# Four rounds of 32 batches in place of five, the routing score moved to GpSimd and PSUM, and a new order of steps

## What is computed

```python
ctx = causal_ema(x, tau_ctx)
gated = x * sigmoid(concat([x, ctx]) @ Wg.T + bg)
h1 = gelu(x @ Wn1.T + bn1)
mod = 0.5 + sigmoid(h1 @ Wn2.T + bn2)                 # one decay rate for each of 128 rows of Wn2
traces = [causal_ema(gated * mod[..., d], tau_raws[d]) for d in range(128)]
temporal = einsum('dbtc,dc->btc', traces, softmax(blend, axis=0))
gate = sigmoid(temporal @ Wtemp.T + btemp)
soma = gelu(x @ Wsoma.T + bsoma)
h = layernorm((soma * gate) @ Wout.T) * gamma + beta

scores = h @ w_router                                 # per batch and time step
top_scores, top_idx = top_k(scores, 16)               # 16 of 32 time steps
update = sigmoid(top_scores) * (gelu(h[top_idx] @ W1 + b1) @ W2 + b2)
out = x + h.at[top_idx].add(update)
```

## Time and profile before

| what | us |
|---|---|
| median of three runs | 192.11 (189.43 to 192.43) |
| the profiled execution | 189.27 |
| its span, first to last instruction | 187.5 |

### The profile page before, as it was taken

The page is one execution under the profiler, slowest core; times in us unless marked ns, Lnnn a source line. Parts: engine busy times, 40 slices in busy tenths (PEclk is TensorE's granted clock), DMA queues, the critical chain, the costliest instruction groups (busy, mean ns, idle before and its releaser), DMA issues.

```text
span 187.5 us, 3480 instructions
## 1 busy us (share of the span) xinstructions
PE 172.6 (92%) x1154; PEld 130.4 (70%) x1154; DVE 143.6 (77%) x223; ACT 96.5 (51%) x177; POOL 134.8 (72%) x158
## 2 busy tenths in 40 slices
PE   5798999999999999999999999999999983994991
PEld 4485445877669588695769687688689943983881
DVE  1628897769997988859787887798789749858822
ACT  3548697264680141772505454578487465157030
...
GB/s 128 167 209 201 0 3 0 0 2 5 0 0 0 3 0 3 0 0 0 3 2 0 0 3 2 0 0 3 2 0 59 0 2 0 112 3 112 0 112 59
DMA packets 12785, 5.62 MB, mean 30 GB/s; under 512 B 2880, under 2 KB 12640, under 8 KB 12768
## 3 DMA queue, kind: packets, MB, share of 16 engines
...
HBM read 3.30 MB, written 2.10 MB: 29 GB/s over the span
## 4 chain that ended last, share of the span: by engine, by line
PE 76%; DVE 11%; issue 3%; POOL 3%; ACT 2%; DMA 2%; ACTq 0%; DVEq 0%; POOLq 0%
PE ring L1042 27%; PE ring L1109 6%; PE ring L1015 5%; PE ring L1026 4%; PE ring L999 4%; PE ring L978 4%; PE ring L1000 4%; PE ring L1049 4%; DVE small L842 3%; PE ring L1057 3%; DVE spread L846 3%; PE ring L1006 2%; PE ring L1032 2%; PE ring L992 2%; PE ring L966 2%
## 5 line engine op out<-in xcount | busy, mean ns | idle before, releaser
L468 POOL TENSOR_TENSOR ctx_acc<-ctx_acc,prod 128x256 f32<-128x256 f32 (+17 forms) x75 | 81.0, 1095 | 30.9 <-DVE prod L817 26.8
L817 DVE TENSOR_TENSOR prod<-ring,gm 128x256 f32<-128x256 f32 (+17 forms) x75 | 41.3, 577 | 8.9 <-PE ring L1042 7.4
L1042 PE MATMUL ring<-mod_hi,decayed_lo 128*128 128x512 f32 (+15 forms) x104 | 35.0, 374 | 0.0
L1042 PE MATMUL ring<-mod_lo,decayed_hi 128*128 128x512 f32 (+15 forms) x104 | 30.1, 326 | 0.0
L1042 PE MATMUL ring<-mod_hi,decayed_hi 128*128 128x512 f32 (+15 forms) x104 | 30.0, 327 | 0.0
L1042 PEld LDWEIGHTS ring<-mod_hi,decayed_lo 128*128 128x128 f32 x104 | 18.4, 189 | 7.6 <-issue 6.3
L1042 PEld LDWEIGHTS ring<-mod_lo,decayed_hi 128*128 128x128 f32 x104 | 19.2, 189 | 2.0 <-issue 1.2
L1042 PEld LDWEIGHTS ring<-mod_hi,decayed_hi 128*128 128x128 f32 x104 | 19.2, 189 | 0.9
L804 DVE TENSOR_TENSOR state<-ring,blend_w 128x1024 f32<-128x1024 f32 x16 | 18.8, 1219 | 1.1 <-PE ring L1015 0.9
L1109 PE MATMUL ring<-w_sb,gm 128*128 128x128 f32 x128 | 15.8, 282 | 0.1
L1109 PEld LDWEIGHTS ring<-w_sb,gm 128*128 128x128 f32 x128 | 15.4, 199 | 0.3 <-issue 0.3
...
## 6 DMA issues: line engine op xcount, KB each, us to landing
x_nat<-in_x_dram SPq DMA_DIRECT2D x3, 512.0 KB, 4.2
out_dram<-x_nat SPq DMA_DIRECT2D x3, 512.0 KB, 3.2
...
```

Source lines behind the costliest of these rows:

```text
L468: nc.gpsimd.tensor_tensor(dst, dst, packed(prod[:, n % NP, 0:width(r)], r, k), ALU.add).then_inc(acc_done, 1)
L817: nc.vector.tensor_tensor(dst, packed(slot(step), r, k), lagged(gated(r), r, k), ALU.mult).then_inc(read(step), 1)
L1042: last = nc.tensor.matmul(to[:, c], w[:, k, :], src[:, c], start=(i == 0), stop=(i == len(parts) - 1))
```

## The change

`QUADS` becomes four rounds of two quads. Round 0 still makes its context by matmul, rounds 1 to 3 scan. The warm-up matmuls stand in three places, five before the first step, one after `turn_b` and four after `turn_a`. The four transfers of `bn1` are issued ahead of the second round's x. The scores' product moves from VectorE to GpSimd, behind the power; the 1e-5 comes in as a 129th column of `squares`, so L480 goes. The `score` step now takes a PSUM bank: VectorE copies the scores into it and spreads them from there, `bc` uses the same bank, and the tanh is copied into it before `pick_w` is made. `normed` scales the tiles first and takes the tanh last. `bias_h` is made after `soft`. The order of steps is new throughout; its last part is shown, of before and of after.

```diff
-QUADS = (1, 2, 2, 2, 1)
+QUADS = (2, 2, 2, 2)
...
-SCANNED = (1, 2, 3, 4)
+SCANNED = (1, 2, 3)
...
-WARM = 3
+WARM = (5, 1, 4)
...
-unit:4.1 normed:1 bc:1 back:3.0 tie:1 down:0 out:2.1 pick:1 sum:3 unit:4.2 stats:2.1 var:2 carry:4.0
-gather:1 unit:4.9 unit:4.8 gate:3 up:1.0 up:1.1 soma_gate:3 score:2 residual:1 scatter:0 normed:2 unit:4.5
-out:3.0 unit:4.11 bc:2 tie:2 turn_pick:1 pick:2 down:1 stats:3.0 unit:4.10 unit:4.6 gather:2 out:3.1
-unit:4.13 back:4.0 unit:4.14 sum:4 stats:3.1 var:3 score:3 up:2.0 up:2.1 scatter:1 gate:4 bc:3 tie:3
-soma_gate:4 normed:3 turn_pick:2 plus_beta:2 pick:3 down:2 plus_beta:3 residual:2 out:4.0 gather:3 stats:4.0
-var:4 scatter:2 turn_pick:3 up:3.0 up:3.1 score:4 bc:4 normed:4 tie:4 pick:4 down:3 plus_beta:4 residual:3
-gather:4 scatter:3 up:4.0 residual:4 up:4.1 turn_pick:4 down:4 scatter:4
...
+decay:0 turn_b:0 powers:0 turn_a:0 context:0 decays:0 xt:0 soft:0 xt:1 rw:0 turn_c:0 turn_d:0 h1:0 h1:1
+context:1 table:0.0 table:0.1 wg:0 mod:0 gated:0 table:0.2 split:0 low:0 table:0.3 wg:1 gated:1 early:0
+soma:0 unit:0.0 plus_beta:0 unit:0.3 unit:0.11 ffn_w:0 nat:0.1 mod:1 unit:0.4 split:1 unit:0.7 unit:0.10
...
+gate:2 up:0.1 score:1 normed:1 soma_gate:2 residual:0 bc:1 carry:3.0 tie:1 pick:1 unit:3.13 down:0 unit:3.6
+gather:1 unit:3.12 back:3.0 sum:3 out:2.0 stats:2.0 out:2.1 up:1.0 stats:2.1 var:2 scatter:0 up:1.1 gate:3
+score:2 bc:2 tie:2 turn_pick:1 soma_gate:3 normed:2 pick:2 down:1 residual:1 out:3.0 stats:3.0 gather:2
+out:3.1 stats:3.1 var:3 scatter:1 plus_beta:2 up:2.0 residual:2 up:2.1 score:3 normed:3 bc:3 tie:3
+turn_pick:2 pick:3 down:2 gather:3 scatter:2 up:3.0 up:3.1 plus_beta:3 turn_pick:3 down:3 residual:3
+scatter:3
...
-        squares = sb("squares", [P, QT, E])
+        squares = sb("squares", [P, QT, E + 1])
...
+        def scores(r, i):
+
+            return slot(("score", r, 0))[:, NT * T + i * NT:][:, 0:tiles(r)]
...
+            for g in range(BT):
+                sp.dma_start(bn1[g * HN:(g + 1) * HN, :], col(b_n1)).then_inc(bn1_in, 16)
             sp.dma_start(bias_in[:, 0:1], col(b_g)).then_inc(bias_inn, 16)
             sp.dma_start(bias_in[:, 1:2], col(b_n2)).then_inc(bias_inn, 16)
             sp.dma_start(tiles_of(x_nat, 1), tiles_of(x_dram, 1)).then_inc(x_in[1], 16)
-            for g in range(BT):
-                sp.dma_start(bn1[g * HN:(g + 1) * HN, :], col(b_n1)).then_inc(bn1_in, 16)
...
                 elif kind == "var":
                     pool.wait_ge(stats_done, nth(last_of("stats", r)))
-                    nc.gpsimd.tensor_scalar(small[:, r % 2, 4, 0:tiles(r)], small[:, r % 2, 5, 0:tiles(r)], 1e-5, None,
-                                            ALU.add).then_inc(own_pool, 1)
-                    pool.wait_ge(own_pool, pool_owned())
-                    nc.gpsimd.tensor_tensor(small[:, r % 2, 7, 0:tiles(r)], small[:, r % 2, 4, 0:tiles(r)],
+                    nc.gpsimd.tensor_tensor(small[:, r % 2, 7, 0:tiles(r)], small[:, r % 2, 5, 0:tiles(r)],
                                             minus_half[:, 0:tiles(r)], ALU.pow).then_inc(rstd_done, 1)
+                    pool.wait_ge(rstd_done, r + 1)
+                    for h in range(QUADS[r]):
+                        pool.wait_ge(read(("out", r, h)), reads_after(("out", r, h)))
+                    nc.gpsimd.tensor_tensor(small[:, r % 2, 6, 0:tiles(r)], o_sb[:, r % 2, 0:tiles(r), E],
+                                            small[:, r % 2, 7, 0:tiles(r)], ALU.mult).then_inc(score_done, 1)
...
                 elif kind == "normed":
-                    act.wait_ge(score_done, r + 1)
-                    made = ("turn_d", 0, 0)
-                    act.wait_ge(read(made), reads_after(made))
-                    nc.scalar.activation(small[:, r % 2, 9, 0:tiles(r)], small[:, r % 2, 6, 0:tiles(r)], ACT.Tanh,
-                                         bias=rsum_h[:, :], scale=0.5).then_inc(sig_done, 1)
+                    act.wait_ge(rstd_done, r + 1)
+                    for h in range(QUADS[r]):
+                        act.wait_ge(read(("out", r, h)), reads_after(("out", r, h)))
                     for n in range(tiles(r)):
                         nc.scalar.activation(o_sb[:, r % 2, n, 0:E], o_sb[:, r % 2, n, 0:E], ACT.Copy,
                                              scale=small[:, r % 2, 7, n:n + 1]).then_inc(norm_done, 1)
+                    made = ("turn_d", 0, 0)
+                    act.wait_ge(read(made), reads_after(made))
+                    act.wait_ge(score_done, r + 1)
+                    nc.scalar.activation(small[:, r % 2, 9, 0:tiles(r)], small[:, r % 2, 6, 0:tiles(r)], ACT.Tanh,
+                                         bias=rsum_h[:, :], scale=0.5).then_inc(sig_done, 1)
...
+            nc.vector.memset(squares[:, :, E:E + 1], 1e-5)
...
-                    dve.wait_ge(bias_inn, 2 * 16)
-                    nc.vector.tensor_scalar(bias_h[:, 0:2], bias_in[:, 0:2], 0.5, None, ALU.mult).then_inc(biases_done, 1)
...
+                    dve.wait_ge(bias_inn, 2 * 16)
+                    nc.vector.tensor_scalar(bias_h[:, 0:2], bias_in[:, 0:2], 0.5, None, ALU.mult).then_inc(biases_done, 1)
...
                 elif kind == "score":
-                    dve.wait_ge(rstd_done, r + 1)
-                    for h in range(QUADS[r]):
-                        dve.wait_ge(read(("out", r, h)), reads_after(("out", r, h)))
-                    s = [small[:, r % 2, i, 0:tiles(r)] for i in range(10)]
-                    nc.vector.tensor_tensor(s[6], o_sb[:, r % 2, 0:tiles(r), E], s[7], ALU.mult).then_inc(score_done, 1)
+                    for former in FORMER[step]:
+                        dve.wait_ge(read(former), reads_after(former))
                     dve.wait_ge(score_done, r + 1)
+                    nc.vector.tensor_copy(scores(r, 0), small[:, r % 2, 6, 0:tiles(r)]).then_inc(own_dve, 1)
+                    dve.wait_ge(own_dve, settled())
                     if r == 0:
                         dve.wait_ge(masks_done, 4 * BT + 2)
                     nc.vector.tensor_tensor(spread[:, 0:tiles(r), :],
                                             eye_t[:, None, :].to_broadcast([P, tiles(r), T]),
-                                            s[6][:, :, None].to_broadcast([P, tiles(r), T]),
+                                            scores(r, 0)[:, :, None].to_broadcast([P, tiles(r), T]),
                                             ALU.mult).then_inc(spread_done, 1)
                 elif kind == "bc":
+                    dve.wait_ge(full(("score", r, 0)), filled(("score", r, 0)))
                     n = tiles(r)
-                    others = slot(step)[:, 0:n * T].rearrange("p (n u) -> p n u", u=T)
-                    same = slot(step)[:, NT * T:][:, 0:n * T].rearrange("p (n u) -> p n u", u=T)
+                    others = slot(("score", r, 0))[:, 0:n * T].rearrange("p (n u) -> p n u", u=T)
                     this = small[:, r % 2, 6, 0:n][:, :, None].to_broadcast([P, n, T])
-                    nc.vector.tensor_tensor(same, others, this, ALU.is_equal).then_inc(own_dve, 1)
                     nc.vector.tensor_tensor(ahead[:, 0:n, 0, :], others, this, ALU.is_gt).then_inc(own_dve, 1)
                     dve.wait_ge(own_dve, settled())
+
+                    nc.vector.tensor_tensor(others, others, this, ALU.is_equal).then_inc(own_dve, 1)
                     dve.wait_ge(own_dve, settled())
...
                     nc.vector.tensor_tensor(pick[:, 0:n, :], rank_of[:, None, :].to_broadcast([P, n, ALL]),
-                                            slot(made)[:, 0:n, None].to_broadcast([P, n, ALL]),
-                                            ALU.is_equal).then_inc(read(made), 1)
+                                            slot(("score", r, 0))[:, 0:n, None].to_broadcast([P, n, ALL]),
+                                            ALU.is_equal).then_inc(pick_done, 1)
                     if r:
                         last = ("turn_pick", r - 1, 0)
                         dve.wait_ge(full(last), filled(last))
-                    dve.wait_ge(read(made), reads_after(made))
+                    dve.wait_ge(pick_done, r + 1)
                     dve.wait_ge(sig_done, r + 1)
+                    nc.vector.tensor_copy(scores(r, 1), small[:, r % 2, 9, 0:n]).then_inc(own_dve, 1)
+                    dve.wait_ge(own_dve, settled())
                     nc.vector.scalar_tensor_tensor(
                         out=pick_w[:, 0:n, :],
-                        in0=small[:, r % 2, 9, 0:n][:, :, None].to_broadcast([P, n, SEL]), scalar=1.0,
-                        in1=pick[:, 0:n, 0:SEL], op0=ALU.add, op1=ALU.mult).then_inc(pick_done, 1)
+                        in0=scores(r, 1)[:, :, None].to_broadcast([P, n, SEL]), scalar=1.0,
+                        in1=pick[:, 0:n, 0:SEL], op0=ALU.add, op1=ALU.mult).then_inc(read(("score", r, 0)), 1)
...
-            for _ in range(WARM):
-                nc.tensor.matmul(ring[:, NBANK - 1, 0:P], ident[:, :], ident[:, :], start=True, stop=True)
```

(52 more changed lines are left out.)

20 lines of the change are left out of this document (3 added, 17 removed).

## The result

The changed kernel takes 182.9 us (median of 4 runs, 182.53 to 183.08) against 191.91 us (189.43 to 192.43) of the kernel before on the same chip. The ratio is 0.957, with a 95% interval of 0.948 to 0.966: 9.0 us faster. A second set of six runs gave 183.11 and 0.955 (0.951 to 0.959). The profiled execution took 182.73 with a span of 180.8; 182.8 and 181.0 had been worked out for them, and 184.5 was forecast for the median.

The account below looks back on a forecast made before the run. TensorE was taken to bound the middle, VectorE's score operations waiting for GpSimd the end. 138.4 + 34.0 + 4.5 + 4.1 gave a span of 181.0 us; the forecast was 184.5, 8 in 10 runs from 179 to 191.

Parts of the forecast that it names:

- What bounds the end: At the end, two small VectorE score operations with two SBUF inputs wait for GpSimd's operation; 9.6 us lost there.
- The second step: Last two rounds: product on GpSimd and spread from PSUM gain 6.8 us, lower clock gone 1.2, together 8.0 of 9.6.
- The third rival: The new copy waits as its predecessors did, 2.3 us in rounds 2 and 3 each: 189 us; chance 0.06.
- kinder than the rule: Rule: GpSimd contends with VectorE's two-SBUF-input or 2-port operations; L757, one SBUF input, took 0.14 us beside GpSimd.
- The tail: Last unit to last scatter: 34.0 us of TensorE work plus 4.5 lost, from 1.6 staying and 2.9 added waiting.
- Head and middle: Up to the last unit: 148.7, moved out -8.3, merged rounds -1.9, context:0 by matmul +1.0, head -1.1: 138.4 us.
- the head's other terms: Head: wait for two ACT copies gone -2.0, larger first x +1.1, ACT's first two copies doubled +0.9 us.
- Warm-up: In context:0, where TensorE was slow, ten warm-up matmuls in three places fill its waits: -1.1 us.
- Middle at no gain and no loss: All other reordering: the middle gets no gain and no loss, bounds -4 to +5 us.
- From span to median: Span 181.0 plus 1.8 outside it gives 182.8 us by difference; by ratio 0.966, 185.5; 184.5 was taken.
- Selections bare: Rival: TensorE stands at bc and gather of rounds 2 and 3, 19.0 us instead of 4.5: 199; chance 0.09.
- The middle paid: Rival: in the middle, two banks for each round's wide lags and GpSimd's lateness cost 5 us: 189.5; chance 0.14.

Follow-up runs that it names:

- each single undoing: Changed kernel with the spread reading from SBUF, without the copy: 186.13 us; changed kernel with the scores' product back on VectorE: 186.37 us.
- The copy into SBUF: Changed kernel with one more copy of the scores, SBUF to SBUF, ahead of the copy into PSUM: 188.01 us, ratio 0.981.
- the last kernel above: Changed kernel with warm-up (8, 1, 0) and the last scatter, add and store in two halves: 181.48 us, ratio 0.947.

## Why the prediction was right or wrong

- **What bounds the end, and the score part: right.** Spread 0.42 in all four rounds, copies 0.17, no granted clock below 1 before the last add, and each single undoing costs: 3.0 and 3.3 us. The second step put 8.0 us on it, all in the tail; in the new order it gave 6.7 there, and another 3.1 in the middle, which the prediction had at nothing. In that 8.0, the 1.2 for the lower clock set a `bc` of 256 columns (1.19) against one of 128 (0.46); after, 256 columns take 0.71, so it is 0.5 for `bc` and 0.5 for `down`.
- **Why the copy doesn't wait: wrong, with the right number.** The step that failed is "which also says that it doesn't wait": L757, a TENSOR_SCALAR on one column, was taken as a price for any operation with one SBUF input. The copy into SBUF took 2.05 to 2.23. The sentence that L757 makes the row "kinder than the rule" falls with it. The third rival had priced such a wait at 189 - 184.5 = 4.5 us, and it came to 4.9. The copy in the change goes through because it writes PSUM, which the prediction says too, in its next paragraph, but its sum went by L757.
- **The tail: 38.5 forecast, 35.7 measured.** Work was 34.0 and is 34.2 by TensorE's busy time. Lost were to be 4.5 and are 1.5: this is the term that was mis-sized most. A part of it came from before, where by the same busy time 7.55 us were lost in this stretch and not 9.6. Power at 1.65 and the hand-over chain from stats to `bc` came out as costed; TensorE's weight load waited 0.55 before `bc:3` instead of 1.7, and TensorE waited 1.3 in two pieces for the bias add (L916), the most in that stretch.
- **After the last scatter: 4.1 forecast, 4.9 measured.** The add grew from 0.69 to 1.23 as said. The other 0.8 is what follows the add, 2.83 before (3.52 - 0.69) and 3.63 after (4.86 - 1.23): the last store now carries 512 KB instead of 256 and lands 3.19 us after its issue instead of 2.45, a transfer that I left out of the moved work. In the last kernel above, with 256 KB in the last store, it is 2.62.
- **Head and middle: 138.4 forecast, 140.2 measured.** TensorE's work up to there fell by 9.8 us (144.88 to 135.05), where -8.3, -1.9, +1.0 and the head's -1.1 make 10.3. Its idle time there rose by 1.3 (3.83 to 5.15), where the head's other terms (-2.0, +1.1, +0.9) cancel. The first unit starts 5.2 us earlier (30.53 and 25.30), since the new order puts more work behind it, and what is gained there says little by itself.
- **Warm-up: wrong.** The step that failed is that the ten matmuls "fill its waits". Six do. The last four stand behind `turn_a`, where TensorE has `context:0` ready: -1.1 as said, +1.7 unsaid, and +0.9 measured. Nor would the -1.1 alone have come through whole: see the wait for `rw` above.
- **Middle at no gain and no loss: nearly.** 1.4 us of waiting appeared. 0.42 of it stands in the records at 32.26, behind L900 held by GpSimd's adds (2.22 us against 0.75), the mechanism of the earlier trace rows in a third place. Another 0.40, at 42.04, is for ScalarE's copy (L535, 1.04) behind the scan (L780, 2.21 on the chain from 38.72), and 0.33 and 0.17 are single waits for VectorE's product and for another such copy.
- **The span: 181.0 forecast, 180.8 measured, in part by luck.** The three stretches missed by +1.8, -2.8 and +0.8 us, and the misses cancel.
- **From span to median: the ratio was the wrong way.** After's runs lie within 0.4 us of its profiled execution; the kernel before runs over 3.0 us, with a median 2.6 above its own. By difference from the profiled execution, 182.8 fits the measured 182.9; 184.5 lay between the two ways. Why the kernel before varies more is open.
- **The rivals.** Selections bare was priced at 199: even with the old score part in the new order, TensorE waited 5.3 us at `bc`, not some 16. The middle paid 1.4 us of the 5 that its rival had.
